# An adaLN block with attention and a mixture of experts: VectorE's base row at the end of its list, TensorE's norm flag read in block 5

## The reference

```
mod = (silu(c) @ wmod)                      # sa, ca, ga, sb, cb, gb; ga and gb kept away from 0
h = layernorm(x) * (1 + ca) + sa
qkv = h @ Wqkv.T + bqkv                     # reshaped to (B, 16 heads, S, 24): q, k, v of 8 each
attn = softmax(q @ k.T / sqrt(8))
x = x + ga * ((attn @ v) @ Wo.T + bo)
h = layernorm(x) * (1 + cb) + sb
probs = softmax(h @ router_w.T)             # 8 experts, the best 2 are taken
topk_w = topk_vals / (sum(topk_vals) + 1e-6)
out = sum over the 2 of (h @ expert_w[id] + prob[id]) * topk_w
x = x + gb * out
```

## Time and profile before

| | |
|---|---|
| runs, median (lowest to highest) | 575.02 us (574.36 to 576.14) |
| profiled execution | 575.76 us, span 574.0 us |
| PE, matmuls busy | 507.4 us (88%) |
| ACT busy | 489.5 us (85%) |
| DVE busy | 374.4 us (65%) |
| POOL busy | 227.7 us (40%) |
| granted PE clock, mean | 0.982 |
| chain that ended last, by engine | PE 61%, DVE 17%, issue 10%, ACT 7% |
| DVE `bias_w`, L1247 | 30 times, mean 1032 ns |

### The profile page before, as it was taken

How to read it: one execution, slowest core, us unless ns; L and a number is a source line. 1 busy time by engine, 2 the same in 40 slices (tenths; PEclk the granted TensorE clock), 3 DMA queues, 4 the chain that set the end, 5 groups by cost and what they waited for, 6 DMA issues and landing times.

```text
span 574.0 us, 19559 instructions
## 1 busy us (share of the span) xinstructions
PE 507.4 (88%) x6667; PEld 195.9 (34%) x6667; DVE 374.4 (65%) x1258; ACT 489.5 (85%) x574; POOL 227.7 (40%) x488
## 2 busy tenths in 40 slices
PE   6879899888888988888898888899888889988987
PEld 6523233323333332333333233333323333332326
DVE  4414566667777666777766677776667777666566
ACT  1378999888889888888988888898888899888975
POOL 1101323345454334545433444543344454334444
PEclk9688999999999999999999999999999999999999
DMA  5563323333223233322323332232333222333000
GB/s 113 150 176 85 90 73 97 94 95 86 73 70 87 74 95 94 85 71 72 86 76 95 94 82 70 76 83 78 95 93 83 69 78 83 81 99 97 21 22 19
DMA packets 83342, 48.25 MB, mean 84 GB/s; under 512 B 59608, under 2 KB 74084, under 8 KB 83300
## 3 DMA queue, kind: packets, MB, share of 16 engines
q1 hardware_dynamic: 68860, 43.30, 28.0%
q10 hardware_dynamic: 14440, 4.38, 3.5%
HBM read 32.78 MB, written 14.87 MB: 83 GB/s over the span
## 4 chain that ended last, share of the span: by engine, by line
PE 61%; DVE 17%; issue 10%; ACT 7%; DMA 2%; SPq 1%; DVEq 1%; ACTq 1%; POOL 0%; POOLq 0%
PE ps_attn L819 26%; PE ps_side L724 18%; PE ps_scores L801 13%; ACT probs L608 7%; DVE bias_w L1247 5%; DVE pair_pw L1245 2%; DVE qkT L1114 2%; DVE weighted L1264 2%; DVE xhat L1100 2%; DVE qk_parts L1123 1%; PE ps_side L747 1%; DMA bo_rows<-in_L_attn_bo_dram 1%; PE ps_scores L676 1%; PE ps_scores L722 1%; DVEq L1253 1%
## 5 line engine op out<-in xcount | busy, mean ns | idle before, releaser
L608 ACT ACTIVATE probs<-ps_scores 128x1024 f32<-128x1024 f32 x512 | 479.8, 1053 | 71.7 <-PE ps_scores L801 70.6
L819 PE MATMUL ps_attn<-probs,values 128*32 128x512 f32 x2048 | 273.5, 601 | 0.1
L801 PE MATMUL ps_scores<-query_stack,key_stack 32*128 32x512 f32 x1024 | 130.6, 498 | 12.8 <-issue 8.1
L801 PEld LDWEIGHTS ps_scores<-query_stack,key_stack 32*128 32x128 f32 x1024 | 49.9, 183 | 229.9 <-ACT probs L608 198.9
L454 POOL TENSOR_SCALAR var_eps<-moments 128x1 f32<-128x1 f32 x64 | 12.3, 192 | 217.8 <-DVE moments L1191 143.0
L724 PE MATMUL ps_side<-experts_in,h2T 128*32 128x256 f32 x896 | 72.3, 390 | 4.0 <-issue 0.9
L1264 DVE TENSOR_TENSOR weighted<-ps_side,coef 128x256 f32<-128x256 f32 x114 | 47.8, 419 | 37.6 <-PE ps_side L724 36.5
L819 PEld LDWEIGHTS ps_attn<-probs,values 128*32 128x32 f32 x2048 | 57.0, 110 | 25.4 <-DVE attn L1174 8.3
L724 PE MATMUL ps_side<-ident,xhat 128*32 128x128 f32 x240 | 13.0, 289 | 38.2 <-DVE weighted L1264 37.2
L505 POOL TENSOR_TENSOR mix<-weighted 128x512 f32<-128x512 f32 x29 | 37.1, 1279 | 3.7 <-ACT weighted L626 3.7
L456 POOL TENSOR_TENSOR rstd<-var_eps,minus_half 128x1 f32<-128x1 f32 x64 | 36.2, 566 | 5.4 <-POOL var_eps L454 0.2
(11 more groups left out here) (185 smaller groups left out, 547.6 us busy)
## 6 DMA issues: line engine op xcount, KB each, us to landing
key_stack<-k_scr SPq DMA_DIRECT2D x128, 128.0 KB, 2.8
query_stack<-q_scr SPq DMA_DIRECT2D x125, 64.0 KB, 2.2
q_scr<-qk_parts SPq DMA_DIRECT2D x94, 64.0 KB, 1.7
k_scr<-qk_parts SPq DMA_DIRECT2D x64, 64.0 KB, 1.7
a_scr<-attn ACTq DMA_DIRECT2D x120, 18.0 KB
sums<-a_scr SPq DMA_DIRECT2D x31, 64.0 KB, 2.1
attnT<-a_scr SPq DMA_DIRECT2D x31, 64.0 KB, 2.2
out_dram<-out_all ACTq DMA_DIRECT2D x28, 64.0 KB, 2.7
```

The source lines that it names most:

```text
L608: nc.scalar.activation(probs[:, k % RING, g, :], ps_scores[:, slot(k, g), :], ACT.Exp, scale=SCALE)\
L801: mm = nc.tensor.matmul(out_, key_stack[p0:p0 + 32, parity, 2 * k:2 * k + 2, :].rearrange("p j r -> p (j r)"), query_stack[p0:p0 + 32, par ...
L819: mm = nc.tensor.matmul(ps_attn[q:q + 32, :], values[:, parity, g, k, :], probs[:, k % RING, g, h * HALF:(h + 1) * HALF], start=(k == 0), ...
```

## The change

The base row leaves its place between xhat and the `weighted` of the first two experts and becomes the last work of DVE's list, behind the `weighted` of the next two. In the last tile it stays where it was, but behind that first `weighted`. `c_x1` gets a wait for the base row of two numbers before, because `x1` has two halves and the base row now reads one of them later.

PE no longer reads the norm flag at the start of a tile. It reads the next tile's flag in block 5, between the side work and weigh, into one of two registers that are held (`bounded_held`), and the tile takes it from there. `reached_apart` puts a wait for a semaphore that was reached long ago in front, so that the register's count stands in a wait of its own.

```
                 if before >= 3:
-                    c_router_base(at[-3], at[-2], 1 - parity)
-
-                if before >= 3:
                     c_weigh(ps_side, at[-2], 1 - parity, 0)
                 if after == 0:
+                    c_router_base(at[-3], at[-2], 1 - parity)
                     c_router_sorted(t - 1)
...
                 if before >= 3:
                     c_weigh(ps_side, at[-2], 1 - parity, 1)
+                if before >= 3 and after:
+                    c_router_base(at[-3], at[-2], 1 - parity)
...
             def c_x1(ps, y1, ring):
                 reached(dve, ev["attn_proj_done"], y1)
                 reached(dve, ev["x_gated_done"], y1)
+                base_before = plus(dve, y1, -2)
+                reached(dve, ev["base_done"], base_before)
...
+            bounded_held = [pe.alloc_register(f"bounded_held_{parity}") for parity in range(2)]
...
-                k_count, q_count, bounded_count = times(pe, at[1], 64), times(pe, at[1], 64), times(pe, at[1], 1)
+                k_count, q_count, bounded_next = times(pe, at[1], 64), times(pe, at[1], 64), times(pe, at[2], 1)
...
-                reached(pe, ev["bounded_done"], bounded_count)
-                flag = pe.value_load(bounded_int[0:1, parity, :], min_val=0, max_val=1)
+                if before == 0:
+                    reached(pe, ev["bounded_done"], 1)
+                    pe.reg_load(bounded_held[0], bounded_int[0:1, 0, :])
+                flag = pe.snap(bounded_held[parity], min_val=0, max_val=1)
...
                     SIDES[k](at, parity, before, after)
+                    if k == 5 and after:
+                        reached_apart(pe, ev["bounded_done"], bounded_next, setup_dve, SETUP_COLUMNS)
+                        pe.reg_load(bounded_held[1 - parity], bounded_int[0:1, 1 - parity, :])
                     if k >= 2:
                         weigh(at[0], at[1], parity, k - 2)
```

## The result

The changed kernel takes 554.79 us (median of 3 runs, 554.44 to 556.58), against 575.02 before: a ratio of 0.9654, 95% interval 0.9614 to 0.9694. The forecast was 558.4 in a range of 545 to 568. The profiled execution has a span of 554.7 us where it was 574.0.

A forecast was written before the change was run, and what follows sets the result against it. PE's 1.50 us wait for VectorE's `weighted` at block 6 bounds the kernel. Per tile pair -2 x 1.58 + 0.73 + 0.99 + 2 x 0.1 = -1.24; twelve pairs -14.9, two tiles behind the loop -1.7: -16.6, 558.4 us, range 545 to 568.

The forecast's parts named there:

- Part 1, the wait of block 6 goes: PE's wait for `weighted` ahead of block 6's side work vanishes; block 6 to 7 falls from 3.46 to 1.88, 1.58 us a tile.
- Rival 2: Block 6's wait stays: GpSimd's `mix` holds the early `weighted`, PE saves 0.88 instead of 1.58; 575 us, chance 0.08.
- 302.4 against 302.47: Block 6: the early `weighted` ends by about 302.4, and PE needs it at 302.47.
- Part 2, the short price: Base row at the end of VectorE's list, where GpSimd rests: `bias_w` takes 0.16 instead of 1.21 us, `base` 0.35.
- Part 2, the late `x1` inside a pass: Next tile's start: `x1` at +3.75 behind block 7's scores against 3.00, block 1's side work at +4.87: 0.73 us lost.
- rival 1: The base row costs nothing at `x1`, and the back edges' 0.40 go too: gain 42.5 us, 532.5 us; chance 0.14.
- Part 2, behind the back edge: At the loop's jump: `x1` at +4.53 behind block 7's scores, block 1's side work at +5.65 instead of +4.66: 0.99 us lost.
- the 0.25 that I put on register instructions: Back edge: three VectorE register instructions on the way to `x1`, put at 0.25 us.
- Part 3, the load: PE's flag load in block 5, between side work and weigh: nearly hidden, taken as 0.1 us a tile.
- the 0.40 at the back edge: Between block 7 and block 0: the flag load's 0.40 us lie inside PE's wait for `bounded` at block 1, adding nothing.
- Rival 3: The load in block 5 drains PE: weigh comes 1.03 us later a tile, 7.6 us slower, 582.6 us; chance 0.10.
- The end: The kernel's last tiles: the first tiles and the last give nothing, since no wait stood there.

The follow-up runs named there:

- experiment 8: Kernel before the change with `pair_pw` and `bias_w` right behind `pair_w`, base row's place unchanged: 537.86 us, ratio 0.9336; with PE's flag load in block 5 as well: 529.81 us.
- Experiment 3: Changed kernel with VectorE's own flag read moved ahead of `norm_max`, reading the next tile's flag into a held register: 536.72 us, ratio 0.935.
- experiment 4: Changed kernel with three flag loads in block 5 instead of one, all used (second form): 559.86 us, ratio 0.9729.
- experiment 1: The base row's move alone: changed kernel with PE reading the flag at the tile's start as before: 554.2 us, ratio 0.9649.
- experiment 2: Kernel before the change with only PE's flag load moved to block 5, base row in its old place: 568.67 us against 573.7, ratio 0.9909.
- 4 (first form): Changed kernel with the same register written three times; its trace has a single load, so it serves as the repeat of the changed kernel: 553.78 us, ratio 0.9648.
- 6: Changed kernel with the last tile's base row ahead of the first `weighted` again, as before the change: 553.16 us, ratio 0.9604.

## Why the prediction was right

It was right in the place, the sign and nearly in the size of each step.

- *Part 1, the wait of block 6 goes:* block 6 to 7 fell to 1.89, forecast 1.88. Rival 2 (the `weighted` held by GpSimd) fell with it: `weighted` started at 324.76, beside GpSimd's `mix` (from 324.72, 1.28 long), and took its 0.42. It ended 0.66 before PE needed it; the forecast's 302.4 against 302.47 was a bound.
- *Part 2, the short price:* `bias_w` 160 ns median, 0.16 forecast; `base` 0.35. It was held by GpSimd before: experiment 8 freed it in the old order and got the gain without the move.
- *Part 2, the late `x1` inside a pass:* forecast at +3.75 behind block 7's scores, measured 331.05 - 327.29 = 3.76 in the tile shown, and 3.80 in the median of the loop (3.74 to 3.93 behind the first pass). Block 1's side work was forecast at +4.87 and came at 332.17 - 327.29 = 4.88. A tile inside a pass was forecast at about 15.8 from block 7 to block 7; it takes 15.65 to 15.84 behind the first pass, where it took 16.5. Experiment 3 shows the cause, the flag read behind the base row; rival 1 (the row is free) fell here.
- *Part 2, behind the back edge:* forecast +4.53 and +5.65, measured 315.37 - 311.02 = 4.35 and 316.50 - 311.02 = 5.48. This term was mis-sized by 0.17 a pass, 2 us: `base` started at +2.44 instead of +2.58, and the rest lies in the 0.25 that I put on register instructions.
- *Part 3, the load:* 0 instead of 0.1 a tile, 2.6 us in all; experiment 4 shows the slack. The claim that the 0.40 at the back edge add nothing here held (experiment 1), and they are real elsewhere (experiment 2). Rival 3 fell: the load did not drain PE.
- *The end:* I gave the last tile nothing. There the base row moved behind `weighted` and made everything behind it 0.7 us late, a step that the sum had left out. In the profiled execution the clock added 1.7.

The sum for the profiled execution was -16.6; measured are 575.76 - 556.58 = 19.2 by the execution's time and 19.3 by the span. Most of the difference lies in the loop. From block 7 of its first tile to block 7 of its last the kernel took 385.9 before and 368.4 after, a gain of 17.5, where the terms of the sum give 14.4 for these 23 steps. Of the 3.1 between them the load makes 2.3 and the back edges about 1.8. Against it stand about 0.9 inside the passes, where the first pass lost 0.4 more than forecast and the others 0.05 each, and 0.3 for a gain of 1.57 instead of 1.58 a tile from block 6 to 7. The remaining 0.2 lie in the other steps.

Outside the loop the sum has 2.2 and 1.8 came out, which is luck: 1.1 ahead of that first block 7 and 3.0 from the last block 7 of the loop to the last scores, less 2.4 at the end. The 3.0 were not taken apart by a run. By the medians of the runs the gain is 20.2, 3.6 more than the sum.

## What to carry to other kernels

A gap of an engine is not its slack: the sequencer may be at work in it, with register loads, checks and jumps, and what counts is how long it then stood at the wait. A chain of small dependent instructions can cost little execution and still stop the sequencer at each inner wait, so that everything behind it starts late. Here it paid to put such a chain where its inputs appear, away from the other engine's long instruction, and to keep the piece at the end of the list free of waits. Before a row is moved, ask which of its instructions is long, and why: here one of them was held by another engine, and moving it and the small one ahead of it was worth more than moving the row.

## What the runs showed of the hardware

The profiled execution of the changed kernel lost 1.7 us to PE's clock near its end. PE had stood idle for 0.73 us for `valsT` and for 1.28 us for `x1hat`. Busy time by stretch (PE busy, PEld, DVE, ACT, POOL, then the granted clock, DMA share and GB/s):

```profile
531.40:536.40 5.00, 2.98 (x34) 1.22 (x38) 3.51 (x14) 2.70 (x3) 1.53 (x4) 0.99 0.05 15
536.40:541.40 5.00, 5.00 (x32) 1.95 (x23) 1.44 (x8) 1.38 (x5) 0.91 (x3) 0.67 0.01 3
541.40:546.40 5.00, 4.74 (x24) 3.47 (x22) 3.90 (x14) 4.22 (x16) 3.28 (x6) 1.00 0.00 0
```

PE was busy for 2.98 of 5 us in the stretch ahead, and in the next the clock fell: a mean of 0.67 says that part of it ran at the lower level, 1.2 GHz. The weigh of the last tile took 3.39 us in the chain of waits:

```profile
536.43 3.39 PE ps_attn L819 x16
```

In experiments 1, 4 (first form) and 6 and before the change the same piece took 1.72. Experiment 1 and the repeat had nearly the same idle time (0.67 and 0.71 for `valsT`, 1.28 for `x1hat`; PE busy for 3.04 and 2.99 of the 5 us) and kept a clock of 1.00. So the drop came in one execution and not in others. Why is open. In the kernel before, the granted clock was full from the fifth of the page's slices on, not from the third: it was 0.86 from 28.70 to 43.05 us and 0.90 from there to 57.40. The steps compared here all lie behind that.

PE's sequencer needed 0.30 us for a register load from SBUF and 0.20 for a compare-and-branch; DVE's needed 0.31 and 0.06 at the back edges shown. DVE's back edge cost 0.6 from the loop's end to the next flag read. Neither shows in an engine's busy time.
